# Fewer neighbour slots for the later hub nodes, five hub chunks for six, and gather halves cut by slots, in a two-layer graph kernel

## What is computed

```
h = max(layernorm(x), 0);  x = x + (adj / clip(sum(adj), 1)) @ h          # layer 0
h = max(layernorm(x), 0)                                                  # layer 1
neigh = (adj > 0) & ~eye;  rank = cumsum(neigh) - neigh;  nb = neigh.sum(-1)
skip = where(nb > 10, (nb + 1) // 2, 1)
rem = neigh & (skip > 1) & (rank % skip == skip - 1) & mask;  rem = rem | rem^T
nd = where(rem, 0, adj with 1 on the diagonal) > 0;  nv = nd.sum(2)
s = sort(where(nd, h of the neighbour, inf))                               # per node and feature
agg = sum over tau, w in (.25,.25), (.5,.5), (.75,.25) of w * interpolate(s, tau * (nv - 1))
x = x + (relu((h + agg) @ W1 + b1) @ W2 + b2) * mask
```

## Time and profile before

| what | value |
|---|---|
| median of 3 runs | 1483.34 us (1483.0 to 1484.73) |
| the profiled execution's own time | 1472.96 us |
| its span, first to last instruction | 1471.0 us |
| mean granted TensorE clock in it | 0.918 of full speed |
| TensorE matmul busy | 1245.2 us |
| VectorE busy | 1157.7 us |
| ScalarE busy | 946.5 us |
| GpSimd busy | 717.5 us |
| HBM read and written | 114.28 and 50.59 MB |

### The profile page before, as it was taken

One profiled execution on the slowest core, in us unless ns is written; L12 is line 12 of the kernel. 1 busy time (PEld: TensorE's weight loads), 2 busy tenths in 40 slices (PEclk: granted clock), 3 DMA queues, 4 the chain that ended last, 5 costly groups with the idle time before them and its releaser, 6 DMA issues.

```text
span 1471.0 us, 30486 instructions
## 1 busy us (share of the span) xinstructions
PE 1245.2 (85%) x11809; PEld 836.6 (57%) x11809; DVE 1157.7 (79%) x2164; ACT 946.5 (64%) x1779; POOL 717.5 (49%) x948
## 2 busy tenths in 40 slices
PE   5879999998989899989999997998999887787441
PEld 4667766775666565656566655765666444454220
DVE  3341499898989799868898989899998689787960
ACT  1677878777778487758577685865876668324210
POOL 0454355534266535754287528762567456402504
PEclk9989999999999999999899999999998999699655
DMA  4455544543254523434343614453254311411000
GB/s 136 130 160 180 170 133 157 164 145 94 80 180 123 166 85 138 135 104 117 111 142 105 206 46 137 135 167 96 69 168 123 113 35 59 131 34 33 15 1 14
DMA packets 119025, 166.99 MB, mean 114 GB/s; under 512 B 58816, under 2 KB 59472, under 8 KB 118864
## 3 DMA queue, kind: packets, MB, share of 16 engines
q1 hardware_dynamic: 103168, 117.72, 27.3%
q0 software_dynamic: 14336, 46.42, 8.3%
q10 hardware_dynamic: 1360, 0.77, 0.2%
HBM read 114.28 MB, written 50.59 MB: 112 GB/s over the span
## 4 chain that ended last, share of the span: by engine, by line
PE 46%; DVE 26%; POOL 9%; issue 8%; ACT 7%; DMA 3%; another core or an unknown queue 1%; ACTq 0%; SPq 0%; POOLq 0%; DVEq 0%
PE psG L612 13%; PE psL L521 9%; PE psT L532 5%; DVE HUB L1197 4%; DVE OHB L1128 4%; DVE HUB L1196 4%; PE psM L658 4%; PE psT L553 2%; DVE OHB L1132 2%; PE psT L557 2%; PE psT L560 2%; ACT RM L800 2%; PE psS L645 2%; PE psT L568 2%; DVE W L1150 2%
## 5 line engine op out<-in xcount | busy, mean ns | idle before, releaser
L612 PE MATMUL psG<-OHB,HL 128*64 128x384 f16 (+5 forms) x3584 | 357.9, 350 | 32.3 <-DVE OHB L1128 16.7
L612 PEld LDWEIGHTS psG<-OHB,HL 128*64 128x64 f16 x3584 | 197.2, 114 | 156.0 <-issue 23.5
L521 PE MATMUL psL<-H0A,AT 128*128 128x65 f32 x2048 | 262.6, 287 | 11.7 <-issue 7.6
L521 PEld LDWEIGHTS psL<-H0A,AT 128*128 128x128 f32 x2048 | 253.4, 202 | 23.6 <-issue 19.9
L1426 POOL DMA_INDIRECT rows<-VR,IDX x128 | 160.2, 1252 | 72.1 <-ACT JUNK L825 39.8
L1196 DVE TENSOR_TENSOR HUB<-HUB 128x1472 f32<-128x1472 f32 (+6 forms) x224 | 179.9, 803 | 18.5 <-ACT HUB L921 15.9
L532 PE MATMUL psT<-UM,NEIT 128*128 128x512 f16 (+3 forms) x1024 | 167.2, 312 | 28.2 <-ACT VR L793 16.2
L819 ACT ACTIVATE VR<-psT 128x512 f16<-128x512 f32 x256 | 147.8, 599 | 56.8 <-PE psT L560 39.3
L1197 DVE TENSOR_TENSOR HUB<-HUB 128x1472 f32<-128x1472 f32 (+6 forms) x224 | 183.0, 817 | 0.0
L1460 POOL DMA_INDIRECT out<-FR x128 | 153.5, 1199 | 37.5 <-issue 36.6
L800 ACT ACTIVATE RM<-VR,SK 128x1024 f16<-128x1024 f16 x128 | 137.7, 1159 | 21.3 <-POOL SK L1377 21.3
...
## 6 DMA issues: line engine op xcount, KB each, us to landing
AT<-in_adjt SPq DMA_DIRECT2D x128, 512.0 KB
RR<-rows SPq DMA_DIRECT2D x128, 288.0 KB
...
rows<-VR,IDX POOLq DMA_INDIRECT x128
out<-FR POOLq DMA_INDIRECT x128
...
```

The lines of the kernel that those rows point to most:

```text
L521: m = e.matmul(ps["L"][:, 65 * t:65 * t + 65], AT[:, n % RING, kk, t * P:t * P + P], H0A[:, T * b + 2 * kp + kk, :], start=(kp == kk == t ...
L612: m = e.matmul(bk[C * b:C * b + C, 0:cols], HL[:, part, (2 * g + b) % 3, k, :], OHB[:, n % 2, b, kk * cols:kk * cols + cols], start=(k == ...
```

## The change

Four things are changed together, and the order string is a new one.

1. **Slots.** Before, all 128 hub nodes had slots 1 to 15, the first 32 had 16 to 31, the first 8 had 32 to 63 and the first 2 had 64 to 127. Now all 128 have 1 to 11, the first 64 have 12 and 13 in pieces of their own and 14 and 15, the first 32 have 16 to 23, the first 16 have 24 to 31, the first 8 have 32 to 47, the first 4 have 48 to 63, and the first 2 have 64 to 95. In columns of one group: 2816 in six chunks (512, 512, 512, 384, 512, 384) became 2304 in five (512, 512, 512, 320, 448). The lists in `HUB` and the merges keep their sizes, so GpSimd zeroes what no gather fills (`empty_slots`, five memsets per group, after the `MARK` write of the group before), and the first merge waits for it.
2. **Halves.** A chunk whose pieces are all single slots (the first three of the hub, the first of `b2a`, and that of `b2b`) is cut in halves by slots and no longer by source tiles (`by_slots`): each half has all eight source tiles for its own columns, so 32 matmuls of 256 columns (or 96) in place of 16 of 512 (or 352), and one VectorE instruction per slot over eight source tiles in place of two over four.
3. **Copies.** Slots that follow each other with the same number of nodes are copied out of a bank by one ScalarE instruction: 11 per group and not 22 for the hub.
4. **Spread pieces.** Pieces with several slots number six and not three, each with two VectorE instructions per half.

The diff, cut to its core:

```diff
--- before.py
+++ after.py
 ORDER = (
-    "XUnnnUUMMAAAUUAWMMUADDDURDMMUADAADDWMMUUDDDDDDRNMAADDDDDTTNBBUNMUBBUgMMABBrrABBUrrrrrrssckssscssssWc"
...
+    "XnnnUUUMAAWAUMMAMRDDUUUAMDDDUDDDMDAAAMWDDDTDDDDMDDUUABRMUTUAABBBBWMMBBBNgrrUrrrrrrNMNsscsskcsUAsUsss"
...
 
 CHUNKS = (
     [[("b1", d, 1, LANES1[d])] for d in range(1, 5)] + [[("b1", d, 1, LANES1[d]) for d in range(5, 8)]]
-    + [[("hub", d, 1, 128) for d in range(d0, min(d0 + 4, 16))] for d0 in (1, 5, 9, 13)]
-    + [[("hub", 16, 16, 32)], [("hub", 32, 32, 8), ("hub", 64, 64, 2)]]
+    + [[("hub", d, 1, 128) for d in range(1, 5)], [("hub", d, 1, 128) for d in range(5, 9)],
+       [("hub", d, 1, 128) for d in range(9, 12)] + [("hub", d, 1, 64) for d in range(12, 14)],
+       [("hub", 14, 2, 64), ("hub", 32, 16, 8), ("hub", 48, 16, 4)],
+       [("hub", 16, 8, 32), ("hub", 24, 8, 16), ("hub", 64, 32, 2)]]
     + [[("b2a", 1, 1, 256), ("b2a", 2, 1, 256)], [("b2a", 3, 1, 160)], [("b2b", 1, 1, 256), ("b2b", 2, 1, 96)]])
-OF = {"b1": [0, 1, 2, 3, 4], "hub": [5, 6, 7, 8, 9, 10], "b2a": [11, 12], "b2b": [13]}
+def by_slots(c):
+
+    pieces = CHUNKS[c]
+    if pieces[0][0] == "b1" or len(pieces) < 2 or any(nd > 1 for _, _, nd, _ in pieces):
+        return None
+    n = max(i for i in range(len(pieces)) if sum(nn for _, _, _, nn in pieces[:i]) <= 256)
+    return pieces[:n], pieces[n:]
+
+
+OF = {"b1": [0, 1, 2, 3, 4], "hub": [5, 6, 7, 8, 9], "b2a": [10, 11], "b2b": [12]}
 GROUPS = {"b1": "b1", "hub": "hub", "b2a": "b2", "b2b": "b2"}
 
 HUB_LANES = 184
 HUB_LISTS = [(0, 56, 128), (16, 12, 32), (32, 46, 8), (48, 2, 8), (64, 54, 2), (80, 10, 2), (96, 44, 2), (112, 0, 2)]
 
+HUB_EMPTY = [(12, 4, 120, 64), (8, 8, 28, 16), (0, 16, 6, 4), (0, 16, 44, 2), (0, 16, 0, 2)]
 HUB_PARTS = [(32, 96, 16), (8, 24, 32), (2, 6, 64), (0, 2, 128)]
-IOTAS = {16: 0, 32: 512, 64: 768}
+SPREAD = [(14, 2, 64), (16, 8, 32), (24, 8, 16), (32, 16, 8), (48, 16, 4), (64, 32, 2)]
+IOTAS = {d: sum(nd * nn for _, nd, nn in SPREAD[:i]) for i, (d, _, _) in enumerate(SPREAD)}
+IOTAS_N = sum(nd * nn for _, nd, nn in SPREAD)
 NETS = {
     "b1": [[(0, 1), (2, 3)], [(4, 5), (6, 7)], [(0, 2), (1, 3)], [(4, 6), (5, 7)], [(1, 2), (5, 6)],
            [(0, 4), (1, 5)], [(2, 6), (3, 7)], [(2, 4), (3, 5)], [(1, 2), (3, 4)], [(5, 6)]],
...
+                parts = by_slots(c)
+                if parts:
+                    first, own = (sum(nn for _, _, _, nn in p) for p in parts)
+                    at, cols = (first, own) if half else (0, first)
+                    for k in range(T):
+                        for part in range(2):
+                            for b in range(2):
+                                m = e.matmul(bk[C * b:C * b + C, at:at + cols], HL[:, part, (2 * g + b) % 3, k, :],
+                                             OHB[:, n % 2, b, k * cols:k * cols + cols], start=(k == 0 and part == 0),
+                                             stop=(k == T - 1 and part == 1), skip_group_check=True)
+                    m.then_inc(p_gm, 1)
+                    return
...
+                runs = []
+                for piece, d0, nd, nn in CHUNKS[c]:
+                    if runs and blk == "hub" and runs[-1][1] + runs[-1][2] == d0 and runs[-1][3] == nn:
+                        runs[-1][2] += nd
+                    else:
+                        runs.append([piece, d0, nd, nn])
                 at = 0
-                for piece, d0, nd, nn in CHUNKS[c]:
+                for piece, d0, nd, nn in runs:
                     if blk == "hub":
-                        for slot, lane, nodes in HUB_LISTS:
+                        for slot, lane, _ in HUB_LISTS:
                             d, nl = max(slot, d0), min(slot + 16, d0 + nd)
-                            if d >= nl or nodes != nn:
+                            if d >= nl:
                                 continue
                             o = at + (d - d0) * nn
                             last = e.activation(
...
+                parts = by_slots(c)
+                if parts:
+                    cols = sum(nn for _, _, _, nn in parts[half])
+                    oh = OHB[:, n % 2, :, 0:T * cols].rearrange("p b (k c) -> p b k c", k=T)
+                    at = 0
+                    for piece, d0, _, nn in parts[half]:
+                        w.wait_ge(t_empty, positions(g, piece, half))
+                        last = e.tensor_scalar(oh[:, :, :, at:at + nn], POS[BLOCKS[piece][0]][:, :, :, 0:nn], float(d0), None,
+                                               ALU.is_equal)
+                        at += nn
+                    last.then_inc(v_oh, 1)
+                    return
...
+                    w.wait_ge(o_zero, g + 1)
...
+            def empty_slots(g):
+                if g:
+                    w.wait_ge(v_ov, g)
+                for d0, nd, n0, nn in HUB_EMPTY:
+                    m = e.memset(L16[0][:, d0:d0 + nd, n0:n0 + nn], 0.0)
+                m.then_inc(o_zero, 1)
+
...
+                elif kind == "slf":
+                    empty_slots(*a)
...
-    cap[:128] = 15
-    for r, slots in ((32, 31), (8, 63), (2, 127)):
+    cap[:128] = 11
+    for r, slots in ((64, 15), (32, 23), (16, 31), (8, 47), (4, 63), (2, 95)):
         cap[:r] = slots
```

More of the change, by code:

```diff
@@ new lines @@
+    "ccSSsscsSSSAcARMUMssscscAAMSSSDDDDhWDlDMRDDDDDDNXDUNDDDDUUNDnnnMMAAAhMTBTUUUBBBBBBBlgfrrrrrrrrAAMsWs"
+    "csskcssssUscssccscssSSSSSSRMUcsMsAAcASSMDDDDDDDWLLDDDDDDFFFMDDDDDTRULLFFFULTLMMBFFFUgBBBLBBLAAdMmdrr"
+    "FFFmeddrrmmBBddrrrrktmmUeLLsssNssssscecddmmAdMNccmddessssssfsmceAUUUccscNVVdSShSAAWASSRmmMUFSSFFdSKm"
+    "dDDDDelMDDDKKAWDLLKDDDDTDDmBMMeKdKKKKKBvDDRDDFBBmdmeFFUrrXTABBBNddmmBLddvUUrgrLrrreroNmNmksesssssssQ"
+    "nssstnsssncFFddFcALLMMscQQtsAtcMccUmQQUFFcAAWdmcmteSSSSSSSSMUFDDdtmRDDddttmDmeLLhDDDDtMtFFUFMMAAUGAW"
@@ new lines @@
+    "tLeLMUtFFFDDDDDGLQQFLRFFUlQQJDJAddDUDDmmTTABQQfBBddBBBmmNMMMrrQBBteerrrrrrNsWssstgJJNLsfsLtktssdsssU"
+    "sdcUmcmccQQscssJSdSSShttMdQAQARDmmQQttMltccdttdUUsFSFMSQeaAtSVtetDVtUttQQFmQLLMcQQAAASvDQQDMQQRdmeFF"
+    "FNdQQNNmDDQQdXmQUUQDDQDdQQQWDDEDDDDDTmUeDDTmndenEdnBLLEABBBBBBBmmvrrMMddmmFMerrrrrrssssAtddssgUscsFF"
+    "ccLcKKWMKKKLKKKAkeUGmmeKKssddEEEAAssssssFFUcSUcEEtSSmSSSoRMGttFmAAMcUDDcttDDLLMddQSSAtDMDDDDFFWUUFmm"
+    "eEeUtEEddDDDDDmtLmtLThADDDDeFFTFBBQQLLRtMMlQQUBBBFFFJJQQQQBBBrrMgAMLrrLWNAUAFFFQrUrQrrNJUsssJJsssssd"
@@ new lines @@
+    "ssALQtdLOOttQssktQtmmscsssNcQQeddmmQcQdAcSfSSdccchSSRmmdMtQdAtcDeUMmmtttttttttttFFFeSQQAUMMSSUeDQlQR"
+    "DDDdXDDmQUdQWDDLQmNdDLDNQQDDDQeDDdDNQQmnDQTQAnnTAVFFFBBBBBBKAmLLMMQMBBQUUFdFgdWrrrrrrrrmmQFsssQQsssa"
+    "fELeAAddkssLescccmmUeVscKddssmmtKKddvcKKKKMcvEESSSmmSssDeeDSSREtDEDEMKGEddAEEoFUFFtMtDtLsLmFFcsEEFmt"
+    "DUUcAAGMeSSKtMWDDDDQDDRDDLLDDddmmDTFtUDQQFUFdAdmQQtmLLQQeBhBFFFQQrAtTMrMBBBBLLUUQBBFQeOMFFLMlgLArarr"
+    "QrWArrttUUssssssssddcNssmOQQmJJAAtddcccNJJAsskfmmeNdedsssstFFFmmccJSSSSQQdtDmdmccDDSSDDDDDQQddDtRMMU"
@@ new lines @@
+    "MSSeQmtetmtthtttAttttttTQQLQWDDLDDDMdDDDdUQRDAUUQQmQQABBTBBelBBBdBQNXmQFdQmrrrfQmFFrrrrrQQWdQgssVVNQ"
+    "QAsQQdssssssssNsssLLEEenEKvnFmKntkmccddvccFcMMeFeUMEUEsMEKKKKKKSSSSLRcLcmmKsEddmEGmSAAeeMEcDUUddDtDD"
+    "DoEUFFSMDAAAttKFGMMDDSSUtWQDDDtDDmTmtLLDEBDDDDUBRBTQdQdFFFQQemLLtMBBBQQmBBrrQQFFFrrrQQddUgrmQtrrmLLA"
+    "AAhkFtlFFLeMLessssFsssQFFJJtscONsssttMddJJtQsLsUmLsssmcNFWFUeAOtMddNcccFJmtmSSSSULUdDDRmedmQQtdMdtQQ"
+    "mmtAMhtQtttcttetMcUedtcdtQLQmSSSSMtADQDQAADDmRQlQFDWQQaDDNQQdfDDQQXdQeDQFFNUULULQTQQQQDDBmDDmBBEEDED"
@@ L63 @@
+    "FFFGtJJJQJJddQQtmmQddQemtmQQtdtdmOLtOLdemmtdemtQttddtFFFttmmeQQQQQQLdeQQQadmQQQFLdQKQQQKQQQFFmmEEEKE"
+    "KdEEdKKffKLLeVmmdemKVeKddFEEEFFvmmvoddKtmmLeeLddFtFFLLmmdetdQQQtQQmmtFFFQQtdtQQdeGmmttQQteJJtQtQQtJt"
+    "JJtQQtttGQQttQttttttttQQtOQEQQQQQQEaOQQQQQQQQQQEEEEEEEEEEEOO"
 )
@@ L402, in program @@
         v_mean, cen_made = sem("v_mean"), (sem("v_cen"), sem("o_cen"))
-        o_diag, o_car, o_thin, o_cls, o_idx, o_x1, o_flag, o_coef, o_fin, o_nv, o_in = (
-            sem(n) for n in ("o_diag", "o_car", "o_thin", "o_cls", "o_idx", "o_x1", "o_flag", "o_coef", "o_fin", "o_nv", "o_in"))
+        o_diag, o_car, o_thin, o_cls, o_idx, o_x1, o_flag, o_coef, o_fin, o_nv, o_zero, o_in = (
+            sem(n) for n in ("o_diag", "o_car", "o_thin", "o_cls", "o_idx", "o_x1", "o_flag", "o_coef", "o_fin", "o_nv", "o_zero", "o_in"))
         f_d, f_p, f_l = sem("f_d"), sem("f_p"), sem("f_l")
@@ L1545, in constants @@
     ch[:, CH_REST] = np.tril(np.ones((P, P)))
-    ci = np.concatenate([np.repeat(np.arange(d0, d0 + nd), nn) for d0, nd, nn in ((16, 16, 32), (32, 32, 8), (64, 64, 2))])
-    ci = np.broadcast_to(ci.astype(np.float16), (P, 896))
+    ci = np.concatenate([np.repeat(np.arange(d0, d0 + nd), nn) for d0, nd, nn in SPREAD])
+    ci = np.broadcast_to(ci.astype(np.float16), (P, IOTAS_N))
     sel = np.zeros((2 * T, COEFS_N), np.float16)
```

45 lines of the change are left out of this document (11 added, 34 removed).

## The result

The changed kernel takes 1436.1 us (median of four runs, 1432.95 to 1443.59) and the kernel before 1483.17 beside it (1471.01 to 1484.73). The ratio is 0.9727, with a 95% interval of 0.9685 to 0.9768: about 40 us less. In the medians it is 47 us. The profiled executions are 1472.96 and 1432.95 us. The forecast was 20 us less, 1463 us, and the range ended at 1440.

A forecast was written before the change was run, and what follows sets the result against it. The prediction took TensorE to bound the long middle, VectorE close behind and bounding the end. The gather's 27 us less and VectorE's net 7 were to land as 20, from 1483.3 to 1463 us, range 1440 to 1482.

The forecast's parts named there:

- What bounds the kernel: TensorE, 92% busy from 150 to 1200 us, bounds the long middle with VectorE (87%) close behind; VectorE bounds the end.
- TensorE's columns: Gather matmuls: 131,072 fewer columns at 0.208 ns give 27 us less; the 1024 extra matmuls cost nothing more.
- the point of loss: Gather's split chunks: above 61 ns per matmul, cutting matmuls in two loses time.
- rival of a price per matmul: Gather's split chunks: at 80 ns per matmul, 50 us more in all, of which 0.53 land: 1510 us, chance 0.03.
- VectorE's one-hots: One-hot columns on VectorE: single slots 32.6 us less, spread pieces 25.3 more, net 7 us less.
- ScalarE and GpSimd: ScalarE's copies 8 us less, mostly hidden; 40 GpSimd memsets at 0.4 us, 16 us, covered by idle time.
- the 3 us that I had set as a mark: GpSimd's wait on the `MARK` write before its memsets was to stay under 3 us per group.
- What lands: Whole kernel: the gather's 27 us land as 14 to 27, VectorE's 7 as 2; 20 us taken, giving 1463.
- 10 us both ways: The new order's effect on all else: no sign in either direction, 10 us either way, 1450 to 1474, chance 0.50.
- more than 10 as a sign of being wrong: The prediction counts as wrong if the order alone moves the time by more than 10 us.
- all of it lands, and the order closes gaps: Rival: TensorE's 27 us give 30, closed idle gaps in the middle 9 more: 1444 us (1436 to 1450), chance 0.20.
- The two slower rivals: GpSimd's wait before its memsets passed on in full, 1490 us, chance 0.08; a price per gather matmul, 1510, chance 0.03.

The follow-up runs named there:

- zero_once: The changed kernel with the memsets and GpSimd's wait ahead of them in the first group alone: 0.9718 of the kernel before, median 1443.3 us.
- three_cuts: The kernel before without 27 us of TensorE matmuls, 21 of VectorE one-hots and 28 ScalarE copies in the hub's first chunks: 0.9894 of before, 1429.6 us.
- late_cut: The kernel before without 24 us of TensorE and 24 of VectorE work in the hub's last chunks: 0.9872 of before, median 1454.8 us.

## Why the prediction was wrong

**What bounds the kernel: wrong, and it is the root.** I read 92% for TensorE and its 46% of the chain as "TensorE is the bound of the long middle part with VectorE close behind". Taking 27 us of its work away alone gave nothing, in the kernel before (1.0038) and nothing that the ratio shows in the changed one (0.9715); at the same granted clock it is 6 us in the kernel before, not 14 to 27. VectorE's is worth about half. The chain names the work that happened to come last at each step. That another path ended a moment earlier at most of them would explain this, and is argued, not shown.

**TensorE's columns: right.** Forecast 27 us less and the gather at 330 us; it is at 332.8, 25 less. The 1024 matmuls more cost nothing, 58 ns each where 61 was the point of loss. The rival of a price per matmul is out.

**VectorE's one-hots: a mis-sized term.** Single slots fell by 24.6 us (132.4 to 107.8) and not 32.6. The spread pieces were to rise by 25.3 us and fell by 5.8, from 79.6 to 73.8. Both sums took the mean of a row for the price of an instruction. In the trace of before, the same eight instructions (four of 1024 elements, four of 512) at two places:

```profile
556.16 3.83 DVE L1132 TENSOR_TENSOR OHB<-POSB,CI 128x1024 f16<-128x1024 f16 x8
...
892.36 6.11 DVE L1132 TENSOR_TENSOR OHB<-POSB,CI 128x1024 f16<-128x1024 f16 x8
```

Start to start, the median instruction takes 0.60 us for 1024 elements and 0.34 for 512, before and now, whether the nodes of a slot are 2, 8 or 64; 256 elements now take 0.20. That makes 0.07 us fixed and not 0.33. Six of the 32 of 512 elements and five of the 32 of 1024 took far longer before, up to 2.17 us in duration for a median of 0.42, and they made the means of 0.547 and 0.756. All eleven lay beside arithmetic of GpSimd for over half of their duration, the others for a fifth on the mean (in the second line above it is an addition of 1.28 us at 894.50). The single slots of 2048 elements have 12 such among 88 in the changed kernel, 7 us over the median together, which covers the 0.73 us in place of 0.67. (The line through the two rows is also 0.079 + 0.301 us per 1024, which gives 0.68, and rows 9 had 2048 elements themselves, at 0.69 and 0.74.) At the medians' prices the spread pieces come to 66 us before and 64 now. VectorE's own terms are 30 us less, of which its busy time shows 18. Part of the rest is in the two merge lines, 11 us longer, whose median instructions are as before: they too have more long ones beside GpSimd. That GpSimd's work is what makes them long is argued from the overlap and wasn't tried.

**ScalarE and GpSimd: right and hidden.** ScalarE has 9 us less (8 forecast), worth nothing. The 40 memsets take 0.35 us each on the mean (0.4 forecast) and are busy for 9.8 us in all (16 forecast). GpSimd stood before them three times for 17.6 us, 11.2 at most, above the 3 us that I had set as a mark; zero_once shows that this costs nothing.

**What lands: the step that failed.** The sum had the work at 20 us, from "The gather's 27 us land with 0.53 (14 us, by the chain) up to 1" and VectorE's 7 "are worth 2", and the new order at nothing, "10 us both ways". The order is the term that misses the time: against the same work in the old order it was worth 22 us (0.9907 to 0.9758), where the forecast itself named more than 10 as a sign of being wrong. The work alone gave 14. The two together are the measured 36 to 40. The granted clock was a term put at nothing without a reason: it rose from 0.918 to 0.922, where the same work in the old order had 0.908. At the same clock the work is worth 22 to 23 us and the order about 7, so the 20 for the work is near, but by luck: TensorE's 27 gave 6 alone, VectorE's share was bigger than forecast (21 us of it less with the slots alone, 18 with the change, not 7), and two errors offset each other. The halves by slots are worth about 5 us in the old order and nothing that is shown in the new. Of the cases, "all of it lands, and the order closes gaps" holds the measured time (1436 to 1450), just, but its TensorE part did not land, and it had 0.20. The two slower rivals did not come about.

**Still open.** Leaving out 27 us of TensorE and 21 of VectorE gave 0.990, and the slots alone, with no more of either, 0.981 beside it; at the same clock 18 and 29 us. ScalarE is not the difference (three_cuts). That the place in the hub is, late_cut leaves possible and doesn't show.
